# First attention layer: weights times values as three float32r products, with the operand splits spread over ScalarE and VectorE

## The reference, cut to what matters

```python
q = (query @ w_q + b_q).reshape(B_, T_, NUM_HEADS, HEAD_SIZE)   # k, v alike
logits = einsum('bthd,bThd->bhtT', q, k) * rsqrt(HEAD_SIZE)
logits = logits - 1e10 * (1.0 - mask)            # mask = (i >= j)
weights = softmax(logits, axis=-1)
attn = einsum('bhtT,bThd->bthd', weights, v)     # "P times V"
out = attn @ w_o + b_o
x = x + out                                      # then x + ffn(layernorm(x)), and so on
```

## Time and profile before

| what | value |
|---|---|
| median of the runs | 839.63 us |
| the profiled execution: its own time | 837.9 us |
| its span | 836.1 us |
| PE busy, share of the span | 775.7 us, 93% |
| DVE busy | 592.8 us, 71% |
| ACT busy | 432.7 us, 52% |
| POOL busy | 277.3 us, 33% |
| granted clock of TensorE, mean | 0.979 |

### The profile page before, as it was taken

The page is one execution under the profiler, slowest core; times in us unless marked ns, Lnnn a source line. Parts: engine busy times, 40 slices in busy tenths (PEclk is TensorE's granted clock), DMA queues, the critical chain, the costliest instruction groups (busy, mean ns, idle before and its releaser), DMA issues.

```text
span 836.1 us, 14186 instructions
## 1 busy us (share of the span) xinstructions
PE 775.7 (93%) x4428; PEld 655.5 (78%) x4428; DVE 592.8 (71%) x1500; ACT 432.7 (52%) x1184; POOL 277.3 (33%) x285
## 2 busy tenths in 40 slices
PE   3999999999999995689999999999999999999963
PEld 2788888888888884368888888888888888888752
DVE  6455554555555448888888878888888788887776
ACT  3555555555555543356656566565565665565320
POOL 6110010101001004535635446356354463553231
PEclk9999999999999999799999999999999999999996
DMA  7010101101010200100100101001001010000001
GB/s 246 1 51 0 50 12 38 50 0 50 0 50 12 63 1 13 51 2 13 51 1 13 50 1 63 0 13 50 0 13 50 12 50 0 13 0 0 1 1 51
DMA packets 23653, 23.74 MB, mean 28 GB/s; under 512 B 2369, under 2 KB 23361, under 8 KB 23506
## 3 DMA queue, kind: packets, MB, share of 16 engines
q1 hardware_dynamic: 23634, 23.51, 8.9%
HBM read 22.45 MB, written 1.05 MB: 28 GB/s over the span
## 4 chain that ended last, share of the span: by engine, by line
PE 87%; DVE 8%; ACT 1%; issue 1%; POOL 1%; DMA 1%; SPq 0%; ACTq 0%; DVEq 0%
PE ps L1247 21%; PE ps L1453 11%; PE ps L1354 6%; PE ps L1252 6%; PE ps L1275 5%; PE ps L1465 3%; PE ps L1318 3%; PE ps L1359 3%; DVE xn L813 3%; PE ps L1490 2%; PE ps L1294 2%; PE ps L1477 2%; PE ps L1507 2%; PE ps L1509 2%; PE ps L1508 2%; PE ps L1466 2%
## 5 line engine op out<-in xcount | busy, mean ns | idle before, releaser
L1247 PE MATMUL ps<-xT_hi,w_hi 128*128 128x512 f32 x256 | 110.2, 431 | 4.4 <-DVE rot L992 2.5
L380 POOL TENSOR_TENSOR w_lo<-w_raw,w_hi 128x512 fp32r<-128x512 f32 x32 | 40.7, 1282 | 217.3 <-ACT w_hi L530 217.3
L1247 PE MATMUL ps<-xT_hi,w_lo 128*128 128x512 f32 x256 | 101.6, 397 | 0.0
L1247 PE MATMUL ps<-xT_lo,w_hi 128*128 128x512 f32 x256 | 101.2, 395 | 0.0
L1022 DVE TENSOR_TENSOR wt<-ps,const 128x384 f32<-128x384 f32 x128 | 68.3, 555 | 41.8 <-PE ps L1466 21.9
L439 POOL TENSOR_TENSOR rot_s<-rot_s,const 128x512 f32<-128x512 f32 x64 | 81.9, 1291 | 16.1 <-ACT rot_s L667 16.1
L574 ACT ACTIVATE wt<-wt,negmax 128x128 f32<-128x128 f32 (+1 forms) x128 | 56.6, 443 | 36.1 <-DVE negmax L889 36.1
L877 DVE TENSOR_TENSOR v<-ps,bv_b 128x256 f32<-128x256 f32 x64 | 26.9, 422 | 59.5 <-PE ps L1252 59.4
L1252 PE MATMUL ps<-wv,xT 128*128 128x256 f32 x256 | 63.1, 380 | 1.0 <-DVE v L877 1.0
L686 ACT ACTIVATE v<-ps 128x256 f32<-128x256 f32 x64 | 24.4, 381 | 73.4 <-PE ps L1453 73.2
L1011 DVE RECIPROCAL enz<-zs 128x128 f32<-128x128 f32 x64 | 60.3, 942 | 0.0
(11 more groups left out here) (160 smaller groups left out, 2140.8 us busy)
## 6 DMA issues: line engine op xcount, KB each, us to landing
w_raw<-a_w_q SPq DMA_DIRECT2D x8, 256.0 KB, 3.2
w_raw<-a_w_k SPq DMA_DIRECT2D x8, 256.0 KB, 3.8
wv<-a_w_v SPq DMA_DIRECT2D x8, 256.0 KB, 2.5
wo<-a_w_o SPq DMA_DIRECT2D x8, 256.0 KB, 3.3
w_raw<-b_Wq SPq DMA_DIRECT2D x8, 256.0 KB, 2.6
w_raw<-b_Wk SPq DMA_DIRECT2D x8, 256.0 KB, 3.3
wc<-b_Wv SPq DMA_DIRECT2D x8, 256.0 KB, 3.5
wc<-b_Wg SPq DMA_DIRECT2D x8, 256.0 KB, 4.0
```

The source lines that it names most:

```text
L380: g.tensor_tensor(lo[:, :, :], raw[:, :, :], hi[:, :, :].bitcast(F32), ALU.subtract).then_inc(ph.w_lo, 1)
L1247: ins = mm(PJ[n[0]], w[:, m, c, h * P:(h + 1) * P], x[:, c, cols], start=(t == 0), stop=(t == len(terms) - 1))
```

## The change

The part of O that covers 256 columns becomes three float32r products: `v_hi * pt_hi + v_hi * pt_lo + v_lo * pt_hi`, where `pt` is the transposed weights and hi/lo are a rounded part and its remainder. The 128-column part stays float32. The parts have to be made: ACT copies `pt_hi` (L599) beside the rest of `wt2` (L600), and `v_hi` (`v_head`); DVE subtracts to get `pt_lo` (`a_pt_tail`) and `v_lo` (`v_tail`). The parts live in buffers of block B (`es_hi`, `es_lo`, `wc_hi`, `wc_lo`), and so the rows name them. Besides, the two halves of the next pair's q and k weights, which ACT rounded at the end of step 0, are now rounded one in step 0 and one in step 1, and POOL's remainders follow, with that of w_o between them.

```diff
             with pool.Fori(0, PAIRS - 1) as i:
                 split_tail(a, i + 1, 0)
+                split_out_tail(a, i, wo)
                 split_tail(a, i + 1, 1)
-                split_out_tail(a, i, wo)
...
+            def v_head(done, b):
+                act.wait_ge(a.proj_evac[done[0]], done[1])
+                s.activation(v_hi[:, b, :], v[:, 2 * b, :], ACT.Copy).then_inc(a_vhi, 1)
...
                         act.wait_ge(a_pt_ps, 2 * (x + b) + h + 1)
-                        s.activation(wt2[:, h, :], X_[h][:, 0:384], ACT.Copy).then_inc(a_pt, 1)
+                        s.activation(pt_hi[:, h, :], X_[h][:, 0:T], ACT.Copy)
+                        s.activation(wt2[:, h, T:T + P], X_[h][:, T:T + P], ACT.Copy).then_inc(a_pt, 1)
...
+                    if b < 2 and not last:
+                        act.wait_ge(a.proj_ps, 2 * NA * i + NA + 2 * b + 2)
+                        split_head(a, i + 1, b)
                     fill(2)
                     fill(3)
-                    if b == 0 and not last:
-                        for m in range(2):
-                            act.wait_ge(a.proj_ps, 2 * NA * i + NA + 2 * m + 2)
-                            split_head(a, i + 1, m)
+                    if rest and b % 2 == 1:
+                        v_head(evacuated(task(NA, i, 4 * b)), 2 * half)
+                        v_head(evacuated(task(NA, i, 4 * b + 2)), 2 * half + 1)
...
+            def v_tail(n, b):
+                dve.wait_ge(a_vhi, n)
+                d.tensor_tensor(v_lo[:, b, :], v[:, 2 * b, :], v_hi[:, b, :].bitcast(F32), ALU.subtract).then_inc(a_vlo, 1)
+            def a_pt_tail(x):
+                for h in range(2):
+                    dve.wait_ge(a_pt, 2 * x + h + 1)
+                    d.tensor_tensor(pt_lo[:, h, :], X_[h][:, 0:T], pt_hi[:, h, :].bitcast(F32), ALU.subtract).then_inc(a_ptlo, 1)
...
                     fill(0)
                     fill(1)
+                    a_pt_tail(x + b)
...
                     (add_y if last else add_group)(a, x + b, b)
+                    if rest and b % 2 == 1:
+                        v_tail(x + b + 2, 2 * half)
+                        v_tail(x + b + 3, 2 * half + 1)
...
                     pe.wait_ge(a_pt, 2 * (x + b) + 2)
+                    pe.wait_ge(a_vlo, x + b + 1)
+                    pe.wait_ge(a_ptlo, 2 * (x + b) + 2)
...
-                        mm(O_[:, o:o + T], v[:, 2 * b, h * P:(h + 1) * P], wt2[:, h, 0:T], start=True, stop=False)
+                        for k, (vs, pt) in enumerate(((v_hi, pt_hi), (v_hi, pt_lo), (v_lo, pt_hi))):
+                            mm(O_[:, o:o + T], vs[:, b, h * P:(h + 1) * P], pt[:, h, :], start=(k == 0), stop=False)
```

More of the change, by code:

```diff
@@ L140, in layer_kernel @@
         es_lo = sb("es_lo", [P, HALF], F32R)
+        v_hi, v_lo = (x[:, :, :].rearrange("p c (t n) -> p (c t) n", n=2 * P) for x in (wc_hi, wc_lo))
+        pt_hi, pt_lo = (x[:, :].rearrange("p (h t) -> p h t", h=2) for x in (es_hi, es_lo))
         sums = sb("sums", [P, 2 * P], F32R)
@@ L187, in layer_kernel @@
         cast_done = sem("cast_done")
+        a_vhi, a_vlo, a_ptlo = (sem("a_" + x) for x in ("vhi", "vlo", "ptlo"))
         gwh_done = sem("gwh_done")
@@ L629, in _ @@
             a_exp_step(0)
+            v_head((0, 3), 0)
+            v_head((0, 4), 1)
             act.wait_ge(small_ld, 16 * 7)
@@ L971, in _ @@
                     a_norm_step(0)
+                if f == 3:
+                    v_tail(1, 0)
+                    v_tail(2, 1)
             with dve.Fori(0, PAIRS - 1) as i:
```

## The result

The changed kernel takes 851.4 us, the median of 4 runs (850.55 to 851.94), against 839.82 us before (4 runs, 838.05 to 842.48): a ratio of 1.0134, 95% interval 1.0106 to 1.0163. It is slower by 11.6 us where 849.5 was forecast, with 853 as the upper end. The profiled execution took 851.47 us, its span is 849.7 us (837.9 and 836.1 before), so the profile has +13.6 us to place.

What follows compares the result with a forecast made beforehand. PE, busy throughout each pair, and an odd-step chain with some 0.06 us slack were taken as the bound; -2.1 + 4.0 + 6.1 + 2.1 = +10.1 us gave 849.5 us, range 842.5 to 853.

Steps and rivals of the forecast that it cites:

- The product: PE's 256-column product in the loop: three float32r passes save 0.15 us in each of 14 even steps, -2.1 us.
- `pt_lo`: Two DVE instructions ahead of the masking delay `o_hi`: +0.29 us in each of 14 odd steps, +4.0 us.
- the rival with 837.5 us: Not slower: the odd-step chain has 0.35 us slack, so all 28 loop steps save 0.15 us; 837.5 us, chance 0.06.
- the dearer chain: DVE held 0.42 us per `pt_lo`, +2.4 us in odd steps, last pair at upper bound; 853.3 us, chance 0.10.
- POOL's remainder over the scales: Step 1 of each of 7 pairs: POOL starts 0.19 us before DVE's scales and holds them, +0.87 us, +6.1 in all.
- The steps: PE's loop steps last 10.0 us (even), 9.3 (step 1) and about 8.4 (step 3), a pair about 37.7 us.
- The last pair: DVE sets the pace there; added remainders delay the output product by 2.1 us, bounds +1.0 and +3.5.
- ACT for nothing: ACT's split copies and added `v_hi` copies fall in idle time and cost nothing; without that cover +4 us.
- The sum: Whole kernel: product, `pt_lo`, POOL and last pair add up to +10.1 us; forecast 849.5 us, chance 0.66.

Runs made afterwards that it cites:

- e10: Changed kernel without `pt_lo` (`v_hi` times `pt_hi` repeated instead) and with both weight halves rounded in step 0 again; 837.41 us, 0.9979 of the kernel before.
- e3: Changed kernel without DVE's `pt_lo`, `v_hi` multiplied by `pt_hi` a second time instead; 843.54 us, 1.0019 of the kernel before.
- e1: Changed kernel with both weight halves rounded at the end of step 0 again, POOL's remainders in old order; 845.83 us, 1.0084 of the kernel before.
- e2: Kernel before with only the weight split spread over steps 0 and 1 and POOL's new order; 846.73 us, 1.0102 of the kernel before.
- e12: Changed kernel with the k weights rounded late in step 1, behind both `v_hi` copies; 848.1 us, 1.0099 of the kernel before.
- e4: Changed kernel with the first head's `pt_lo` moved ahead of the second v bias; 845.3 us, 1.0081 of the kernel before.
- e9: Changed kernel with the last pair kept on the float32 product, without `pt_lo` and `v_lo` there; 847.0 us, 1.0097 of the kernel before.
- e5: Changed kernel with the k weights rounded early in step 1, right behind `wo_hi`; 847.58 us, 1.0113 of the kernel before.

## Why the prediction was right, point by point

- *The product, -0.15 us per even step.* Measured -0.13 (10.17 to 10.04), 14 times -1.8 in place of -2.1. The passes pace at 0.12. The Trainium skill ("TensorE: Matmul & The Clock Gate", section "The mechanism") has a sentence by which loads overlap only in other row groups; rows 123.19, 123.31, 123.43 of after and e10 disagree with it, as the earlier trace rows did. The same section of the Trainium skill also lets a load be pulled ahead when it goes to the background weight buffer, which the prediction left out; with that the rows are no contradiction. Which of the two holds here no row tells.
- *`pt_lo`, +0.29 in each odd step.* Step 3 is +0.28, `o_hi` +0.34 (forecast +0.35). e3 and e10 put the instructions themselves at 0.33 or 0.34; against before, 0.05 of the product's saving comes off. 14 times 0.28: +3.9 in place of +4.0. That the chain had next to no slack was right, and so the rival with 837.5 us fell; so did the dearer chain, since DVE's two took 0.75 us, and the next one started 0.67 behind the first, as the forecast had it.
- *POOL's remainder over the scales, +0.87 in step 1.* The mechanism is shown by e1, e2 and e12, and the lead was forecast at 0.19 and is 0.23 to 0.24 us. The size is 0.67 or 0.68. The transposes came 1.45 us behind the scale's due time and not 1.64: the scales ended 0.35 and not 0.4 behind POOL, and the 0.11 us that was put between weight load and matmul does not stand in the rows (both start at 128.14). Step 2 grew by 0.05 besides, in every kernel in which POOL met the scales of the first head (after, e2, e3, e4, e9) and in none of the others. It stands in the first transpose: after PE's wait of some 0.5 us the second follows it by 0.165 us and not 0.109 (the three take 0.55 at 128.14, 0.49 in the earlier trace rows). In sum +5.1 (e1 against after) in place of +6.1. The Trainium skill ("SBUF — State Buffer", section "SBUF: two separate sides") has whichever engine starts first hold the port for its whole instruction. e12 fits this: the scale that was running when POOL began kept its length (0.34 us), and the next one waited for POOL. That POOL waited for the running scale is hardly seen: its row is 1.33 us long, 0.04 more than in after. So the holder changes between DVE's own instructions, and all four scales are not one block. At the start of the kernel the rows do not fit the rule (last section), and the earlier trace rows showed only one order of the two.
- *The steps.* Forecast 10.0, 9.3, 10.0, 8.4 and a pair of 37.7 us; measured 10.04, 9.07, 10.09, 8.39 and 37.60 (263.17 over 7).
- *The last pair, +2.1.* The chain was followed rightly: +0.88, +0.86, +2.77 and +2.75 us at its four points (forecast +0.9, +0.89, +2.84 and +2.84), and +2.36 at the output product. With the clock undisturbed the whole is +2.06 (e12). What was not seen is that the clock may fall ahead of that product: another 1.3 us, +3.4 in the profiled execution of after, inside the bounds of +1.0 to +3.5. It did in after, e1, e4 and e5, but also in e2, whose last pair is the old one, and not in e12, so that it comes with the changed code is not shown.
- *ACT for nothing.* Step 0 has ACT busy 6.22 us of 10.04 and is 0.13 shorter; its cover held.
- *The sum.* Forecast +10.1; the loop's +7.2 and the last pair's +3.4 make +10.6 against +11.6 by the medians. The two misses (POOL 1.0 us too dear, the last pair 1.3 too cheap for its clock) nearly cancel, and that 849.5 came within 2 us of 851.4 is in part luck of that kind: the mechanisms were right, their sizes off by as much as the whole miss. In the profiled execution 3.0 us remain, 0.5 at the start and 2.4 from block B on, in code that is unchanged. For the medians the remaining 1.0 us cannot be placed.

## What to carry to other kernels

Before work is added to an engine that is half idle, look up what stands behind it in its own order and whether that has any slack: two VectorE instructions cost 0.33 us per odd step where both stood behind one v bias, and nothing where one of them stood ahead of it (e4). Where VectorE scales from SBUF to SBUF on the way to TensorE, a GpSimd instruction of 1.29 us that comes 0.2 us before it makes the scale 0.86 us longer and the step 0.67, and one that comes 0.4 us behind the first of two scales that TensorE waits for costs nothing (e12). A saving in every step is worth only what the same change does not spend at the seams: the product saved 2.5 us of the loop (e10), and the chain of the last pair alone gave back 2.1. And a saving of 0.3% (2.5 us) is looked for in the steps: code that is the same in all these kernels varied by 5 us from one execution to another.

## What the runs showed of the hardware that was not expected

At the start of the kernel four scales of DVE, SBUF to SBUF, start almost together with a row of POOL's operations. In the kernel before:

```profile
13.13 6.86 DVE L813 TENSOR_SCALAR xn<-acc,mv,rstd 128x256 f32<-128x256 f32 x4
13.15 1.28 POOL L380 TENSOR_TENSOR w_lo<-w_raw,w_hi 128x512 fp32r<-128x512 f32 x1
...
17.08 1.81 POOL L403 MEMSET accT<- 128x2048 f32 x1
```

In the profiled execution of e5, where code and data of this part are the same:

```profile
11.79 3.76 DVE L828 TENSOR_SCALAR xn<-acc,mv,rstd 128x256 f32<-128x256 f32 x4
...
11.95 1.38 POOL L383 TENSOR_TENSOR w_lo<-w_raw,w_hi 128x512 fp32r<-128x512 f32 x1
```

The four take 6.86 us where DVE begins 0.02 us ahead of POOL and 3.76 where it begins 0.16 ahead. In the kernel before, the first scale by itself is recorded with 5.90 us, to 19.03: it ends 0.14 us behind the last of six POOL operations that follow each other without a gap (this remainder and five MEMSETs, to 18.89). Each scale takes 0.4 us when nothing is beside it. So POOL's operations, one right behind the other, can keep DVE out for more than one of their lengths, and DVE's row does so although it starts first. In e5 the first scale is through in 0.41 us, and the other three end one by one, each some 0.15 us behind one of POOL's operations.

e5's loop starts at 27.36 us, 6.0 earlier than before. Of this, 3.1 us are the four scales. Another 1.0 stands earlier: the two scales of the earlier trace rows at 8.47 take 0.74 us in e5, where POOL's remainder comes only behind their start. The rest, 1.9 us, is spread over the transfers at the beginning and the work behind the scales, and was not taken apart. In the other eleven profiles the loop starts between 32.6 and 34.8 us. e5's runs reach from 841.89 (the profiled one) to 849.08 us; whether such a start is what spreads the runs of all the kernels was not tested.
